# Attention inside two mixture-of-experts passes: the q and k parts written to memory once, repeated by eight loads

## The reference, cut to what matters

```python
def reference(x, ...):
    x = x + 0.5 * ffn(layernorm(x))
    x = x + attn(layernorm(x))
    x = x + 0.5 * ffn(layernorm(x))

def attn(x):                       # 16 batches, T = 256, 16 heads of 8
    q, k, v = split(x @ W_attn + b_attn, 3)
    att = einsum('bhqd,bhkd->bhqk', q, k) / sqrt(8)
    att = softmax(where(causal, att, -inf))
    return einsum('bhqk,bhkd->bhqd', att, v) @ W_proj + b_proj
```

## Time and profile before

| | |
|---|---|
| median of 3 runs | 856.14 us (853.59 to 862.99) |
| the profiled execution | 855.18 us, its span 853.3 us |
| PE, DVE, ACT, POOL busy | 61%, 60%, 37%, 39% of the span |
| memory read, written | 47.25 MB, 41.94 MB |
| DMA queue q1 (issued by SP) | 59.86 MB, 22.7% of the 16 DMA engines' time |

### The profile page before, as it was taken

The page is one execution under the profiler, slowest core; times in us unless marked ns, Lnnn a source line. Parts: engine busy times, 40 slices in busy tenths (PEclk is TensorE's granted clock), DMA queues, the critical chain, the costliest instruction groups (busy, mean ns, idle before and its releaser), DMA issues.

```text
span 853.3 us, 19461 instructions
## 1 busy us (share of the span) xinstructions
PE 518.0 (61%) x6235; PEld 351.6 (41%) x6235; DVE 510.1 (60%) x2626; ACT 314.9 (37%) x602; POOL 334.3 (39%) x332
## 2 busy tenths in 40 slices
PE   2323159978566968696859979645532799309400
PEld 2222148856433534353435535323321588108300
DVE  6837348847755757575657978636145588007822
ACT  1001138846333535353535534212111588007300
POOL 2875730053454352535243121334267101750274
PEclk9999999979969989898999988758565799659855
DMA  9911125534636151515151541000011355214332
GB/s 292 296 52 59 51 70 141 148 91 126 192 115 204 35 189 53 173 38 187 46 181 36 165 158 42 23 28 33 19 37 56 96 149 144 65 49 131 112 91 61
DMA packets 107239, 90.30 MB, mean 106 GB/s; under 512 B 11026, under 2 KB 99475, under 8 KB 106771
## 3 DMA queue, kind: packets, MB, share of 16 engines
q1 hardware_dynamic: 72850, 59.86, 22.7%
q0 software_dynamic: 8192, 16.79, 6.4%
q10 hardware_dynamic: 26112, 12.59, 5.0%
HBM read 47.25 MB, written 41.94 MB: 105 GB/s over the span
## 4 chain that ended last, share of the span: by engine, by line
issue 33%; PE 28%; DVE 17%; another core or an unknown queue 11%; POOL 4%; ACT 2%; DMA 2%; SPq 1%; DVEq 0%; ACTq 0%; POOLq 0%
PE banks L1502 11%; DVE by_token L773 6%; PE banks L1513 5%; PE banks L1490 4%; POOL by_token L483 3%; DVE mparts L778 1%; PE banks L1292 1%; DVE mraw L773 1%; PE banks L1436 1%; PE banks L1268 1%; PE banks L1242 1%; SPq L434 1%; DVE xnT L754 1%; PE banks L1217 1%
## 5 line engine op out<-in xcount | busy, mean ns | idle before, releaser
L773 DVE CUSTOM_DVE_ANT_0 by_token<-banks,konst_sb 128x128 f32<-128x128 f32 (+1 forms) x512 | 147.1, 353 | 66.7 <-issue 66.2
L533 POOL DMA_INDIRECT rows_by_expert<-by_token,posi x120 | 116.9, 974 | 100.8 <-DVE posi L959 66.4
L1502 PE MATMUL banks<-xT,pT 128*64 128x128 f32 x1536 | 117.8, 295 | 36.6 <-ACT xT L712 21.2
L605 ACT ACTIVATE pT<-banks 128x1536 f32<-128x1536 f32 x64 | 92.8, 1450 | 65.7 <-PE banks L1270 62.9
L1502 PEld LDWEIGHTS banks<-xT,pT 128*64 128x64 f32 x1536 | 90.8, 146 | 58.9 <-issue 49.2
L706 ACT ACTIVATE pT<-w_experts 128x384 f32 x192 | 90.0, 517 | 50.9 <-remote 25.1
L483 POOL DMA_INDIRECT by_token<-results_by_tile,tilepos x64 | 61.1, 955 | 118.3 <-DMA results_by_tile<-ysb 99.4
L483 POOL DMA_INDIRECT yg<-results_by_tile,tilepos x64 | 61.7, 964 | 71.7 <-DMA results_by_tile<-ysb 53.3
L1107 DVE SCALAR_TENSOR_TENSOR sig<-banks,sig 128x256 f32<-128x256 f32 x96 | 40.5, 422 | 66.5 <-ACT sig L716 37.4
L1513 PE MATMUL banks<-pT,gT 128*64 128x128 f32 x768 | 64.9, 284 | 14.2 <-issue 11.5
L1124 DVE TENSOR_TENSOR ysb<-banks,w_experts 128x128 f32<-128x128 f32 x192 | 46.8, 284 | 36.0 <-remote 21.6
(11 more groups left out here) (161 smaller groups left out, 1013.4 us busy)
## 6 DMA issues: line engine op xcount, KB each, us to landing
xt<-rows_by_expert SPq DMA_DIRECT2D x192, 64.0 KB
results_by_tile<-ysb ACTq DMA_DIRECT2D x96, 128.0 KB
q_stack<-q_by_part SPq DMA_DIRECT2D x8, 1024.0 KB
k_stack<-k_by_part SPq DMA_DIRECT2D x8, 1024.0 KB
q_by_part<-q_parts SPq DMA_DIRECT2D x16, 384.0 KB, 3.3
k_by_part<-k_parts SPq DMA_DIRECT2D x16, 384.0 KB, 3.4
x_resident<-in_x SPq DMA_DIRECT2D x8, 256.0 KB, 5.8
w_experts<-in_w_gu SPq DMA_DIRECT2D x1, 2048.0 KB
```

What stands on the lines that cost most here:

```text
L533: pool.indirect_dma_start(out=rows_dram, out_offset=bass.IndirectOffsetOnAxis(ap=posi[:, c:c + 1], axis=0), in_=rows_of(f, q)[:, i, :], in ...
L605: nc.scalar.activation(pT[:, s % 2, :], banks[:, 3:6, :].rearrange("p a q -> p (a q)"), ACT.Exp, scale=SCALE).then_inc(a_exp, 1)
L773: last = nc.vector.tensor_tensor_reduce(masked[:, (3 * g + qt) * P:(3 * g + 2 * qt + 1) * P], of, lag, 1.0, NEG * NEG_BELOW, ALU.add, ALU. ...
L1502: last = nc.tensor.matmul(bank[2 + k % 2][h * HALF:(h + 1) * HALF, at:at + P], w_tile[:, 2 * k + i, which * F + h * HALF:which * F + (h + ...
```

## The change

The memory tensor of a stack holds three parts instead of eight copies. One store per stack writes the parts as they are, and eight loads, one for each combination p, fill partitions p, p+8, p+16 and so on (16 partitions, 128 KB each). Each load picks the part of its combination by the tables `Q_LEVEL` and `K_LEVEL`. The loads of q are issued before SP waits for the low part of k. The counts in the waits on `a_spread` and `a_stack` change with the number of DMAs.

```diff
-        stack_dram = [[nc.dram_tensor(f"{n}_by_part{i}", (P, PARTS, QUAD * P), BF16, kind="Internal").ap() for i in range(2)] for n in "qk"]
+        stack_dram = [[nc.dram_tensor(f"{n}_by_part{i}", (P, 3, QUAD * P), BF16, kind="Internal").ap() for i in range(2)] for n in "qk"]
...
-            for which in range(2):
+            for which, level in enumerate((Q_LEVEL, K_LEVEL)):
 
                 sp.wait_ge(a_low[which], x + 1)
                 if which == 0 and not first:
 
                     sp.wait_ge(a_st, scored)
-                src, dst = parts[which], stack_dram[which][half]
-                if which == 0:
-                    for a in range(2):
-                        sp.dma_start(dst[:, 3 * a:3 * a + 3, :], src[:, a:a + 1, :].to_broadcast([P, 3, QUAD * P])).then_inc(a_spread[0], 16)
-                    sp.dma_start(dst[:, 6:8, :], src[:, 2:3, :].to_broadcast([P, 2, QUAD * P])).then_inc(a_spread[0], 16)
-                else:
-                    for a in range(2):
-                        sp.dma_start(dst[:, 3 * a:3 * a + 3, :], src[:, :, :]).then_inc(a_spread[1], 16)
-                    sp.dma_start(dst[:, 6:8, :], src[:, 0:2, :]).then_inc(a_spread[1], 16)
-            for which in range(2):
-                sp.wait_ge(a_spread[which], x * 48 + 48)
-                sp.dma_start(stack[which][:, half, :, :], stack_dram[which][half].rearrange("(m r) p t -> (r p) m t", m=H // 2)).then_inc(a_stack[half], 16)
+                by_part = stack_dram[which][half]
+                sp.dma_start(by_part, parts[which][:, :, :]).then_inc(a_spread[which], 16)
+                sp.wait_ge(a_spread[which], x * 16 + 16)
+                of_head = by_part.rearrange("(m r) a t -> r m a t", m=H // 2)
+                for row in range(PARTS):
+                    sp.dma_start(stack[which][row:P:PARTS, half, :, :], of_head[:, :, level[row], :]).then_inc(a_stack[half], 16)
...
-                beyond_first(act, a_spread[which], x * 48)
+                beyond_first(act, a_spread[which], x * 16)
...
-                    pe.wait_ge(a_stack[v // 2], (t + 1) * 32)
+                    pe.wait_ge(a_stack[v // 2], (t + 1) * (2 * PARTS * 16))
...
+Q_LEVEL = (0, 0, 0, 1, 1, 1, 2, 2)
+K_LEVEL = (0, 1, 2, 0, 1, 2, 0, 1)
```

## The result

The changed kernel takes 870.99 us (median of 4 runs, 869.81 to 874.22), the kernel before 858.31 us beside it (4 runs, 853.59 to 862.99). The ratio is 1.014, 95% interval 1.010 to 1.018: slower by 12.7 us, where a gain of 1.4 us was forecast and 868 us was the end of the range. The profiled execution took 871.53 us, its span 869.7 us, which is 16.4 us over the profiled execution of before.

What follows compares the result with a forecast made beforehand. PE was taken to wait for a stack only at pair 0 (2.82 us), pair 6 having little room. From 855.18 us, -1.4 for pair 0 and 0 elsewhere gave 853.8 us; range 844 to 868.

Steps and rivals of the forecast that it cites:

- c: Cost of one of the sixteen new stack loads issued by SP: taken as 0.5 us, own range 0.41 to 0.73.
- pair 0: First pair, whose stack PE awaits for 2.82 us: stack forecast at T + 15.0 against T + 16.4, gaining 1.4 us.
- T + 7.5 + 15c: Time the last stack load lands: three landings of 2.5 us plus the sixteen loads' cost, the last c inside its landing.
- T: Start of q's first store on SP, from which the stack's chain is counted; 222.72 in pair 0 of the earlier trace.
- Pair 6: Pair without a gather in front, stack needed at T + 17.4: no change at c = 0.5, 1.1 us wait at 0.73.
- Everything else costs nothing: ACT's wait for stores, SP's queue and the unchanged PE, DVE and POOL programs were to add 0 us.
- the cover of pairs 1 to 5: Previous pair's units and idle beside POOL's gathers hide the chain: 26.5 us in pair 2, no wait up to c = 1.27.
- POOL's own last issue: Claimed end of PE's five idles beside the gathers, at most 7.1 us each: POOL's last indirect DMA, unaffected by SP's DMAs.
- Slower: the small loads are dear: Rival: sixteen short loads hold up SP, hitting pairs 0 and 6; over 1% from c = 0.91, 872.4 us at 1.2; chance 0.14.
- Faster: Rival: thinner stack traffic shortens PE's idles beside gathers, at most 35 us, down to 820 us, or the expert tail; chance 0.11.
- The change doesn't do what it says: Rival: reads repeat as before, so if loading alone sets landings, pair 0 gains zero; inside the forecast, no separate chance.
- the forecast's half rate: Upper end of c: stack loads run at half of 359 GB/s, 0.73 us per 128 KB, giving +3.2 us, 858.4.

## Why the prediction was wrong

**"I take c = 0.5, near the issuing rows."** Mis-sized. c is 0.645 us: 0.600 of issuing and 0.045 between two loads. It lay inside the prediction's own range of 0.41 to 0.73, but pair 0 was said to lose from 0.59. I had named SP's issuing as the lower end and taken it from rows for other shapes (333 and 371 ns). The shape matters: 16 partitions in steps of eight 0.60 us, 128 partitions with the same bytes 0.43. This is worth 15 x 0.145 = 2.2 us in the formula.

**"T + 7.5 + 15c."** The form was right, its landings were not. Measured for pair 0: q's store lands after 2.7 us, q's loads take 5.2, k's store lands after 3.7, k's loads take 5.1, and the last lands 5.2 us after SP is through (239.25 to 244.43). That makes T + 21.9, against T + 15.0 by the forecast: 2.2 from c, 4.1 from the landings (11.6 against 7.5), and 0.6 since the last load's issue is not part of its landing. I took the shortest landing of the trace, 2.5 us, three times; the same row gave 3.4 as its median and 5.2 as its longest. Pair 0 lost 5.3 us instead of gaining 1.4, which the two kernels without gathers confirm at 5.3. In part the last landing is late because POOL's gathers (232.4 to 242.2) run beside it: in later pairs the gathers add about 1 us, as shown above. That the rest, some 1.6 us over the 3.6 of a later pair, comes from the last expert stores is argued only: every kernel here kept both beside pair 0.

**Pair 6: "With c = 0.5 nothing changes; with 0.73 PE waits 1.1 us."** Right in mechanism: PE waits 0.68 us, between the two.

**"Everything else costs nothing" and the cover of pairs 1 to 5.** Here the prediction failed by most. On the chip of the forecast no stack is waited for in these pairs, as it said, but about 7 us go all the same. They did not appear without gathers. The runs show that more DMAs alone cost something (eight loads in place of one, 0.59%, pair 0 included; fourteen tiny ones per pair, 0.45%, hardly clear of noise), and that fewer bytes gave nothing back that can be seen. I had ruled it out with "POOL's own last issue, which no DMA of SP holds back". In the changed kernel the idles end 1.65 to 2.18 us after that last issue, but in the unchanged kernel on another chip they end 0.3 to 1.7 us after it, so this coincidence belonged to one execution. PE waits there for its own `a_s_low`, whose count arrives late. The reading "POOL's own last issue" took what happened at the same time for the cause. Why the count is late beside gathers stays open, and so does how the 7 us divide between the number of DMAs, k's loads falling beside the gathers (before, SP had issued pair 2's last load at 305.59, ahead of them), and the chip.

**The cover was a stall.** The 26.5 us from T to the use of pair 2's stack counted PE's 7 us idle as cover. On chips of the other kind the idle does not exist: the cover is about 17.5 us, the chain takes 21.0, and the change costs 3.0% to 3.6% instead of 1.4%. With the gathers spread it is shorter still: in the kernel before, PE was free for pair 2 at T + 13.2 (312.11 - 3.03 - 295.92).

**The rivals.** *Slower: the small loads are dear* was the right mechanism, held up by SP's issuing, with pair 0 its first victim; I priced a loss of over 1% from c = 0.91, and 0.645 was enough, since the landings and the idles came on top. *Faster* was right that the idles belong to the gathers, and that most of 35 us can be had: 44 us without gathers, 21 us with the same gathers spread. That the stack's bytes have to do with it found no support: 10.5 MB fewer gave nothing back. *The change doesn't do what it says* is excluded by the bytes.

The prediction held that no row showed the rule of the port swizzle (SBUF — State Buffer of the Trainium skill, section "Door 1: The DMA port swizzle"), by which these loads reach eight of the sixteen ports. The runs agree with the rule: with loads queued the engines were full at 204 GB/s, against 356 GB/s before, so 128 KB take 0.64 us where the forecast's half rate gave 0.73. In the changed kernel the issuing every 0.645 us comes to the same, so this limit shows only where loads queue up. That the ports are the reason was not tested apart. The same skill's page DMA: Bandwidth & Descriptors, section "Issuing engines are not separate DMA queues", calls the time to initiate a DMA "usually small relative to the DMA itself". For these loads it is not: 0.60 us of issue stands against the 0.365 us that 128 KB take at the rate of the earlier trace rows, or the 0.64 us that they take in this shape.

**What would have shown it.** Of the signs named, only the bytes came out in full. The idle before the first scores was 8.52 us and not under 2.82, the loads stood 0.645 us apart and not 0.4 to 0.5, pair 6 had an idle, and four of the five idles beside gathers grew by more than 1.25 us (3.1, 2.1, 1.7 and 1.3 us). This last was a bad test, since the unchanged kernel alone differs by as much from chip to chip. The one on the loads' spacing (0.9 us or more) was set too far out.

## What to carry to other kernels

Before one large load is cut into many, multiply the number by the issue time of that shape, not of the nearest load in the trace, and add a whole landing, at its median or longer, for each link of the chain; bytes saved are worth nothing once issuing sets the rate. Look at the share of the DMA engines beside the GB/s: full engines at a low rate mean that the shape, and not the bytes, is the limit. Cover that consists of another engine's stall is not cover to build on: it differs between chips and goes when the stall is mended. Where PE stands beside a block of POOL's indirect DMAs, spreading the block over several units can pay (2.25% for the kernel before, on one chip), provided that nothing behind them on POOL is needed soon.

## What I had not expected of the hardware

The unchanged kernel took 661 to 670 us on three chips and 854 to 874 us on the others, at granted clocks of 0.89 to 0.91 and 0.81 to 0.84. Every trace of the second kind has PE standing for 5.7 to 9.1 us beside the blocks of eight indirect DMAs, where the kernel has them, while no trace of the first kind has that. What PE stands for is a count of its own matmul, which came 5.7 to 9.2 us late in the two profiles of the comparison and 0.02 us late in that of the kernel before on the other kind. Leaving the gathers of the pairs out gained 44 us on the one kind (864.67 to 820.48) and lost 6.5 us on the other (665.00 to 671.47). The idle beside gathers is thus under a quarter of the 200 us between the kinds; the rest was not looked for. Nothing in the program differs, and what differs between the chips, or between the times at which they ran, was not found.
